# Decoder layer on one core: attention's keys and queries transposed by DMA, issued from SyncE, in place of TensorE

## The reference, cut to what matters

```python
x = x + ssm(layernorm(x), ...)              # mixer; 8 batches of 256 tokens, 512 channels
x = x + xattn(layernorm(x), ctx, ctx)       # 32 query heads on 8 key heads of 16 channels
x = x + moe(layernorm(x), ...)              # 8 experts, top 2

qh = q.reshape(b, s, KVH, G, D).transpose(0, 2, 3, 1, 4)
kh = k.reshape(b, s, KVH, D).transpose(0, 2, 1, 3)
scores = jnp.einsum('bkgsd,bktd->bkgst', qh, kh) * scale
attn = jax.nn.softmax(scores, axis=-1)
out = jnp.einsum('bkgst,bktd->bkgsd', attn, vh)
```

## Time and profile before

| | us |
|---|---|
| median of three runs | 1481.68 (1474.73 to 1482.41) |
| the profiled execution | 1481.74 |
| its span | 1479.9 |
| mean granted TensorE clock | 0.945 |

### The profile page before, as it was taken

How to read it: one execution, slowest core, us unless ns; L and a number is a source line. 1 busy time by engine, 2 the same in 40 slices (tenths; PEclk the granted TensorE clock), 3 DMA queues, 4 the chain that set the end, 5 groups by cost and what they waited for, 6 DMA issues and landing times.

```text
span 1479.9 us, 22910 instructions
## 1 busy us (share of the span) xinstructions
PE 1333.3 (90%) x7672; PEld 734.5 (50%) x7672; DVE 870.6 (59%) x1819; ACT 724.2 (49%) x1390; POOL 584.9 (40%) x859
## 2 busy tenths in 40 slices
PE   6589999999999998998787778884999999999997
PEld 4456666666666665654233333332444444444443
DVE  4887887979797978757887888645111111111111
ACT  2476667767666776662676767652111111111110
POOL 2345564555455456674223345143122222222221
PEclk9899999999999999997899988875999999999999
DMA  9000000000000000000200000002343444344322
GB/s 330 12 8 6 6 7 1 12 1 12 1 11 2 8 6 8 16 1 1 97 33 33 34 33 31 29 31 72 114 128 65 121 129 129 58 129 128 58 44 29
DMA packets 40276, 73.00 MB, mean 49 GB/s; under 512 B 18529, under 2 KB 22881, under 8 KB 39137
## 3 DMA queue, kind: packets, MB, share of 16 engines
q1 hardware_dynamic: 30224, 48.10, 9.3%
q0 software_dynamic: 8736, 20.61, 7.5%
q10 hardware_dynamic: 1200, 2.82, 0.5%
HBM read 148.91 MB, written 19.99 MB: 114 GB/s over the span
## 4 chain that ended last, share of the span: by engine, by line
PE 65%; DVE 19%; issue 5%; DMA 4%; POOL 3%; ACT 3%; SPq 0%; POOLq 0%; ACTq 0%; DVEq 0%
PE work_ps L533 11%; PE gate_ps L1502 9%; PE up_ps L1502 9%; PE down_ps L1488 9%; PE work_ps L605 7%; DVE conv L814 7%; PE work_ps L538 4%; PE work_ps L627 3%; DVE maxes L1204 3%; PE work_ps L1030 2%; PE mturn_ps L538 2%; DVE mix L730 2%; PE decay_ps L1021 2%; PE decay_ps L615 2%; DMA x_sb<-x_dram 2%
## 5 line engine op out<-in xcount | busy, mean ns | idle before, releaser
L533 PE MATMUL work_ps<-xnT,w_in 128*128 128x256 f32 (+1 forms) x1216 | 301.7, 393 | 1.3 <-ACT xnT L639 0.8
L730 POOL TENSOR_TENSOR mix<-decay,cbm 128x512 f32<-128x512 f32 x128 | 183.0, 1431 | 214.4 <-ACT decay L725 177.4
L533 PEld LDWEIGHTS work_ps<-xnT,w_in 128*128 128x128 f32 (+1 forms) x1216 | 220.5, 189 | 64.1 <-issue 33.3
L721 ACT ACTIVATE decay<-decay_ps 128x512 f32<-128x512 f32 x256 | 154.3, 603 | 112.2 <-PE decay_ps L615 109.7
L1590 POOL DMA_INDIRECT out_dram<-y_out,ids x39 | 61.9, 1587 | 336.0 <-DVE row_w L1554 232.3
L1204 DVE TENSOR_REDUCE maxes<-work_ps 128x2 f32<-128x512 f32 x256 | 166.6, 683 | 44.9 <-PE work_ps L1006 44.0
L814 DVE SCALAR_TENSOR_TENSOR conv<-raw,conv_w,conv 128x256 f32<-128x256 f32 x240 | 180.5, 757 | 6.9 <-ACT conv L681 1.1
L1102 ACT ACTIVATE prob<-decay_ps 128x512 f32<-128x512 f32 x256 | 142.7, 607 | 79.9 <-PE decay_ps L1021 79.0
L1569 DVE TENSOR_TENSOR act<-gelu,up_ps 128x512 f32<-128x512 f32 x39 | 26.8, 687 | 253.9 <-PE up_ps L1502 253.9
L725 ACT ACTIVATE decay<-decay 128x512 f32<-128x512 f32 x256 | 164.1, 641 | 4.7 <-PE work_ps L533 3.0
L1502 PE MATMUL gate_ps<-w_e,xgT 128*128 x312 | 142.2, 599 | 2.0 <-ACT xgT L1519 1.6
(11 more groups left out here) (268 smaller groups left out, 1898.9 us busy)
## 6 DMA issues: line engine op xcount, KB each, us to landing
w_e<-c_experts_dram SPq DMA_DIRECT2D x39, 3072.0 KB
normed_tokens<-r_xn SPq DMA_DIRECT2D x17, 256.0 KB, 2.1
out_dram<-x_sb SPq DMA_DIRECT2D x17, 256.0 KB, 2.6
x_sb<-x_dram SPq DMA_DIRECT2D x1, 3584.0 KB, 22.4
w_in<-c_w_inT_dram ACTq DMA_DIRECT2D x1, 2560.0 KB, 12.0
w_in<-c_w_inT_dram SPq DMA_DIRECT2D x1, 2048.0 KB, 8.6
w_out<-c_w_outT_dram SPq DMA_DIRECT2D x1, 2048.0 KB, 13.6
RT<-cum_scratch SPq DMA_DIRECT2D x32, 48.0 KB
```

Of the source, the lines that this page charges most:

```text
L533: m = e.matmul(ps[0:width, at:at + L], w_in[:, k, col:col + width], xnT[b % 2][:, k, :], start=(k == 0), stop=(k == KD - 1))
L721: e.activation(decay[s % 5][:, :], decay_ps[s % 3][:, :], ACT.Relu, scale=-1.0).then_inc(piece_done[stage], 1)
L730: return e.tensor_tensor(four(mix[s % 5]), four(decay[s % 5]), cb, ALU.mult)
```

## The change

The pieces `k_turn`, `k_copy`, `q_turn`, `q_copy_v` and `q_copy_s` go, on TensorE, VectorE and ScalarE. In their place SyncE issues one transposing DMA per 128x128 fp16 block, from the staging tile straight into `kT` or `qT`: 8 in `k_flip` and 16 in `q_flip`, for each tile. The first max sweep of a batch waits for all 48 of them. The staging pieces move 8 slots earlier, the context load 6 slots, the blocks take about the slots of the turns less 8 to 10. SyncE gets a wait `freed` of its own ahead of its first block, for the last z projection and the last x gate.

```diff
+DMA_ONLY = {... "k_flip", "q_flip"}
     for b in range(NB):
         r = n * (b - 2)
         if b:
-            put(r - 12, ("ctx_in", b))
+            put(r - 18, ("ctx_in", b))
         if b and b % 2 == 0:
             for t in range(2 * TPB):
-                put(r + t, ("q_bn", b * TPB + t))
-            put(r + 4, ("q_stats", b // 2))
-            put(r + 5, ("q_newton", b // 2))
+                put(r - 8 + t, ("q_bn", b * TPB + t))
+            put(r - 4, ("q_stats", b // 2))
+            put(r - 3, ("q_newton", b // 2))
         for t in range(TPB):
             if b:
-                put(r + 2 + 2 * t, ("k_hi", b, t), ("k_lo", b, t))
-                put(r + 10 + 4 * t, ("q", b, t))
-                put(r + 11 + 4 * t, ("q_hi", b, t), ("q_lo", b, t), ("q_dup", b, t))
-            put(r + (10 if b else 16) + 2 * t, ("k_turn", b, t))
-            put(r + (10 + 1 if b else 17) + 2 * t, ("k_copy", b, t))
-            put(r + 15 + 5 * t, ("q_turn", b, t, 0))
-            put(r + 17 + 5 * t, ("q_copy_v", b, t, 0), ("q_turn", b, t, 1))
-            put(r + 19 + 5 * t, ("q_copy_s", b, t, 1))
+                put(r - 6 + 2 * t, ("k_hi", b, t), ("k_lo", b, t))
+                put(r + 2 + 4 * t, ("q", b, t))
+                put(r + 3 + 4 * t, ("q_hi", b, t), ("q_lo", b, t), ("q_dup", b, t))
+            put(r + (2 * t if b else 16 + 2 * t), ("k_flip", b, t))
+            put(r + (7 + 4 * t if b else 15 + 5 * t), ("q_flip", b, t))
...
                 if p == 0:
-                    e.wait_ge(*done("k_copy", b, 1))
-                    e.wait_ge(*done("q_copy_v", b, 1, 0))
-                    e.wait_ge(*done("q_copy_s", b, 1, 1))
+                    for i in range(TPB):
+                        e.wait_ge(load_k[i], 16 * KVH * (b + 1))
+                        e.wait_ge(load_q[i], 16 * NPR * (b + 1))
...
+            elif stage == "freed":
+                e.wait_ge(*done("z", NB - 1, NCZ // 2 - 1, 1))
+                e.wait_ge(*done("x_gate", NB - 1, PAIRS[-1]))
...
+            elif stage == "k_flip":
+                b, t = key
+                e.wait_ge(*done("k_lo", b, t))
+                if b >= 3 and t == 0:
+                    e.wait_ge(*done("score", N_ITEMS * (b - 2) - 1))
+                for k in range(KVH):
+                    e.dma_start(kT[b % 3][:, k, t * P:(t + 1) * P], k_st[t][:, k, :, :].rearrange("p a s -> p (a s)"), transpose=True).then_inc(load_k[t], 16)
+            elif stage == "q_flip":
+                b, t = key
+                e.wait_ge(*done("q_lo", b, t))
+                e.wait_ge(*done("q_dup", b, t))
+                for k in range(NPR):
+                    e.dma_start(qT[b % 3][:, k, t * P:(t + 1) * P], q_st[t][:, 2 * k:2 * k + 2, :].rearrange("p a s -> p (a s)"), transpose=True).then_inc(load_q[t], 16)
```

More of the change, by code:

```diff
@@ L171, in mixer_slots @@
     return slots
-DMA_ONLY = {"freed", "mixed", "cum_out", "cum_in", "ctx_in", "n_out", "router_in", "first_expert", "r_store", "out_in", "c_weight_out"}
+DMA_ONLY = {"freed", "mixed", "cum_out", "cum_in", "ctx_in", "n_out", "router_in", "first_expert", "r_store", "out_in", "c_weight_out", "k_flip", "q_flip"}
 def bank_use(stage, *key):
@@ L183, in bank_use @@
         return ("y", *unit), ("yz", *unit)
-    if stage == "q_turn":
-        return (stage, *key), ("q_copy_s" if key[2] else "q_copy_v", *key)
     if stage == "product":
@@ L188, in bank_use @@
         return ("pv", *group), ("pv_copy", *group)
-    read_by = {"k_turn": "k_copy", "n_turn": "n_copy", "pv_turn": "pv_out", "r_turn": "r_copy", "r_logit": "r_keep", "c_count": "c_slots", "max": "max_fold", "xn_turn": "xn_copy", "dt": "dt_exp", "dt_turn": "dt_tok", "cb": "cb_mask", "x_turn": "xdt", "state": "state_copy",
+    read_by = {"n_turn": "n_copy", "pv_turn": "pv_out", "r_turn": "r_copy", "r_logit": "r_keep", "c_count": "c_slots", "max": "max_fold", "xn_turn": "xn_copy", "dt": "dt_exp", "dt_turn": "dt_tok", "cb": "cb_mask", "x_turn": "xdt", "state": "state_copy",
                "expand": "expand_copy", "carry": "carried", "ones": "rstat"}
@@ L340, in layer_kernel @@
         store_cum, load_ctx, load_max = (semaphore(n) for n in ("store_cum", "load_ctx", "load_max"))
+        load_k = [semaphore(f"load_k{t}") for t in range(TPB)]
+        load_q = [semaphore(f"load_q{t}") for t in range(TPB)]
         load_cum = [semaphore(f"load_cum{c}") for c in range(TPB)]
@@ L984, in tensor_attention @@
                 e.wait_ge(*done("x_add", NT - 1))
[L985 to L996, removed]
             elif stage == "max":
@@ L1072, in scalar_attention @@
                 if b:
-                    e.wait_ge(*done("k_turn", b - 1, t))
+                    e.wait_ge(load_k[t], 16 * KVH * b)
                 e.activation(k_st[t][:, :, :, 0:DH], both, ACT.Copy)
@@ L1088, in scalar_attention @@
                 if b:
-                    e.wait_ge(*done("q_turn", b - 1, t, 1))
+                    e.wait_ge(load_q[t], 16 * NPR * b)
                 e.activation(q_st[t][:, :, 0:DH], a_xn[t][:, :].rearrange("p (h d) -> p h d", d=DH), ACT.Copy).then_inc(piece_done[stage], 1)
[L1091 to L1096, removed]
             elif stage == "exponent":
@@ L1188, in vector_attention @@
                 variance_guess(e, own, a_mv, a_rows, ts).then_inc(piece_done[stage], 1)
[L1189 to L1198, removed]
             elif stage == "max_fold":
```

## The result

The changed kernel takes 1750.8 us (median of four runs, 1748.7 to 1755.2) against 1480.1: a ratio of 1.181, 95% interval 1.177 to 1.185. The profiled execution spans 1747.9 us, 268.0 more than before.

What follows compares the result with a forecast made beforehand. No engine was full before, the attention being a chain of hand-overs; after the change SyncE's block issues would bind it. Stalls of 49 + 9 + 186 + 4 = 248 us on 1481.74 gave 1730 us, range 1500 to 2180.

Steps and rivals of the forecast that it cites:

- The price d: Time on SyncE from one transposing block's issue to the next one's, taken as 1.25 us; 384 blocks in all.
- the qT row: Profile row of the existing SBUF DMA into qT: SyncE busy 0.574 us, landing 1.8 us after issue.
- the cumulative sums' segments: 256-byte segments moved between 577.7 and 584 us: 17.5 ns a segment, giving 0.14 us a block on the DMA engines.
- (a): First max matmul, today at 649.88, waits for batch 0's 48 blocks, issued from 637.06: 49 us of stall.
- (b): Batch 1's first max waits for its blocks, SyncE ending last: 9 us more.
- (c): Batches 2 to 7, six periods: SyncE's blocks stretch the period from 36.9 to 67.8 us, adding 186 us.
- (d): Nine constant loads and the first expert's weights stand once between batch 2's blocks: 4 us.
- (e): After batch 7's first max, today about 922 us, nothing changes.
- The removed work: Transposes and copies gone: 2.7 us a batch, 16 us over six, plus 4 in the lead-in; hidden in the forecast.
- My two small-d rivals: Cheaper blocks: d of 0.5 to 0.9 gives 1535 us, chance 0.22; d at most 0.48 gives 1469 to 1474, chance 0.14.
- The case given 0.46: The forecast itself: d between 0.9 and 1.7 us, time 1603 to 1902 us, chance 0.46.
- The case of the other side: A block costs what a plain DMA does, d at most 0.48; SyncE's queue hides: 1469 to 1474 us, chance 0.14.

Runs made afterwards that it cites:

- the merged run: The changed kernel with one transposing DMA per tile for all eight key blocks and one for all sixteen query blocks, 4 issues a batch: 1492.8 us, ratio 1.0067.
- e6_late: One transposing DMA per key or query tile, with stagings and context load at the slots of the kernel before: 1478.8 us, ratio 0.9971; run again, 1480.1 us, ratio 0.9975.
- e8: The kernel before with only the keys by DMA, one transposing DMA per tile, queries still by TensorE and copies: 1484.05 us, ratio 0.9999.
- e11: The kernel before with only the queries by DMA, one transposing DMA per tile, keys still by TensorE and VectorE: 1477.4 us, ratio 0.9961.
- e7: As e6_late, but TensorE still does all the old transposes into a PSUM bank nobody copies; results unused: 1486.15 us, ratio 1.0019.
- e9: The changed kernel with the context load 9 slots earlier from batch 2 on, ahead of the previous batch's query blocks on SyncE: 1761.45 us.
- e2: The changed kernel with the key and query blocks of batches 3 to 7 left out, scores taken from operands of batches 0 to 2: 1607.6 us.
- e1: The kernel before with only the stagings 8 slots and the context load 6 slots earlier, turns and copies at their old slots: 1488.95 us, ratio 1.0036.

## Why the prediction was right

**What binds.** SyncE's issue, one block after another: confirmed by its timeline without gaps among a batch's 48 blocks, by TensorE's wait for the blocks at every batch's first max, and by the merged run, which removes issues and moves the same bytes. That a first block takes 1.11 to 1.22 us with nothing ahead of it speaks against a full queue as the reason.

**The price d.** 1.25 us was taken, 1.27 measured between issues. The number was right, the reason wrong, so that it came so near is luck. I took the qT row's landing less its issue, on the argument that issues overlap and movement does not. It is the other way round: the movement overlaps (DMA share 0.12, 0.13 us for a further block in one DMA), and SyncE's 1.23 us does not. The 0.14 us a block that I worked out from the cumulative sums' segments was close to that 0.13; I should have trusted it, and asked what SyncE does per instruction. The 1309 ns that the Trainium skill, page "VectorE: DVE Perf Modes", section "The three transpose paths", gives for a block lies near the 1232 ns issue; whether it means the same thing no run here shows. (By it the sum would have been 384 x 0.059 = 23 us longer, not some 25.) Had I kept my own reason, I would also have expected whole-tile DMAs to change nothing.

**The stalls.** (a) first max: 49 us forecast, 52.6 measured. A context load that I had not put there holds the first block back to 639.17 (2.1 us), the 48 blocks take 62.1 us rather than 60, and the max matmul follows 1.2 us after the last issue's end, not 1.8. (b) batch 1: 9 against 13.1; the blocks were longer again, and SyncE stood 1.4 us (722.7 to 724.07) before the query blocks, most of it waiting for POOL's staging: the queries were ready at 724, not at the 715 of the prediction. (c) and (d) the period: 67.8 against (1194.49 - 766.74) / 6 = 71.3 us, so 190 forecast and 206 measured. The blocks take about 61.9 us rather than 60; from a first max to the next key block it is 7.5 to 7.7 us in batches 3 to 7, where I had 6; the step behind the blocks is 1.2 us instead of 1.8; and the constants take 5.2 us once instead of 4. (e) after batch 7's first max: nothing forecast, -3.9, cause open. Sum 248 forecast, 268.0 measured: 20 us more than predicted, mostly because the time between issues and the hand-over before the key blocks were each put a little short.

**The removed work.** The step that failed, though it did not enter the forecast: "the worth lies between 0 and 4.2 us; I take the middle one", 16 + 4 us together. Where SyncE is free, the runs show less: e6_late and its repetition are 3 to 5 us faster than before, e8 not at all, e11 by about 6. The unblocked period did not fall to 34.2: in e6_late six rows of maxima take (924.81 - 698.59) / 6 = 37.7 us each, against 36.9 before. The gain there is lies in the lead-in, where the first row of maxima is issued at 698.59 instead of 703.87. It goes with the query copies of VectorE and ScalarE: from the start of the last z projection to that row 68.7 us pass before and 68.2 in e8, which keeps these copies, but 64.1 in e11, 63.8 in e6_late and 64.6 in its repetition, which do not; with the turns put back and the copies left out (e7) it is 65.6. These are single executions. So some 3 of those 4 to 5 us come without taking anything off TensorE. My two small-d rivals used 34.2 and 36.9 and so came out short: with plain copies, 0.64 us from one to the next, their sum gives 1481.7 + 20 + 6 x 1.6 + 4 = 1515 us, and 1534 was measured. The missing 19 us lie in the periods, 42.2 us against the 38.5 of that sum.

**The waits.** The context load, held back on SyncE, was costed at nothing, and that stands: e9 shows that it lay beside the landing. But I had not named that ScalarE would wait 194 us for it.

**The chances.** The case given 0.46 happened. The case of the other side breaks even, by its own terms, near d = 0.56 us and not near 0.5: there the stall of 48d - 11 and six times 48d + 7.8 - 34.2 make up the 20 us of removed work. Even a plain copy of a block takes 0.64 from one to the next, and the 20 us weren't there.

## What to carry to other kernels

Count instructions on the issuing queue before bytes: a queue that issues n DMAs a period at d us each is an engine with a busy time of n x d, and the table of busy times does not show it. Here a whole key tile in one transposing DMA costs SyncE about what one 128x128 block does, and a query tile of sixteen blocks some 0.7 us more in the median. So the change as made loses 18%, and the same change with 4 DMAs instead of 48 is even or a little better. And price work taken off TensorE by what its waits say, not by its length: where the granted clock sinks and the hand-overs stay, most of it is not given back.

## What was not expected of the hardware

- A transposing DMA from SBUF to SBUF takes SyncE 1.23 us to issue, twice a plain one of the same block (0.60), 1.29 for 8 blocks and 1.3 to 1.9 for 16. Landing grows from 2.4 us to 3.3 and 4.3.
- The granted clock in the attention (740 to 960 us) went from 0.88 to 0.77 when 25 us of transposes over six batches went, to 0.82 with them put back unused beside the DMAs, and stood at 0.86 with the stagings merely moved. With the turns back it is still below before, while the DMA share is 0.27 instead of 0.10; whether the traffic has a part in that stays open. The fall itself does not need the traffic: e2 has neither turns nor blocks in the window below, and its granted clock is 0.79 at a DMA share of 0.08.

```profile
845.00:1095.00 250.00, 190.98 (x1240) 80.78 (x1239) 171.66 (x450) 150.66 (x287) 80.56 (x205) 0.79 0.08 29
```

- With the turns gone and no blocks at all (e2, batches 3 to 7) the five periods average 42.2 us, against 38.0 for the same five with the turns on TensorE. The early staging goes with 1.6 us of it (e1: (936.52 - 738.31) / 5 = 39.6). The rest goes with the clock: over these five periods 233 matmuls fewer keep TensorE busy 160.6 us instead of 151.7, at a granted clock of 0.76 instead of 0.90. Which of the two, the lower clock or the longer period, brings the other was not tested.
